# Denominators as jobs on three PSUM banks, register queries staged ahead, bias rows as latent columns, in a two-attention fp32 kernel

## The reference

```
xn = layernorm(h)
# A: latent attention, 8 heads, no mask
c_q, c_kv, k_r = xn@W_DQ + b_DQ, xn@W_DKV + b_DKV, xn@W_KR + b_KR     # 32 columns each
q = [c_q@W_UQ + b_UQ | c_q@W_QR + b_QR];  k = [c_kv@W_UK + b_UK | k_r]
a = softmax(q k^T / sqrt(160));  out_A = (a @ (c_kv@W_UV + b_UV)) @ W_O + b_O
# B: 16 heads of 16, keys masked
q, k, v = xn @ W_qkv
sim = mean over heads of cos(g, q), scaled to 0..1 over all tokens;  pos = sim > 0.9
x_pos, x_neg = attention over the keys with pos / without (the first 5 tokens are keys in both)
rows with pos take x_pos, the others x_neg; the first 5 rows (register) take the mean of both
out = h + out_A + out_B @ W_proj + b_proj
```

## Time and profile before

| | us |
|---|---|
| runs shown (3): lowest, median, highest | 3069.21, 3077.69, 3081.52 |
| profiled execution: its time | 3083.09 |
| its span, first to last instruction | 3081.3 |
| busy: PE, DVE, ACT, POOL | 2900.2, 2256.7, 1676.5, 1428.3 |
| idle of PE ahead of `rs`, until Z was in (8 times) | 14.8 |
| mean granted clock of TensorE (1 is 2.4 GHz) | 0.976 |

### The profile page before, as it was taken

One profiled execution on the slowest core, in us unless ns is written; L12 is line 12 of the kernel. 1 busy time (PEld: TensorE's weight loads), 2 busy tenths in 40 slices (PEclk: granted clock), 3 DMA queues, 4 the chain that ended last, 5 costly groups with the idle time before them and its releaser, 6 DMA issues.

```text
span 3081.3 us, 45461 instructions
## 1 busy us (share of the span) xinstructions
PE 2900.2 (94%) x16898; PEld 1283.4 (42%) x16898; DVE 2256.7 (73%) x4085; ACT 1676.5 (54%) x1947; POOL 1428.3 (46%) x680
## 2 busy tenths in 40 slices
PE   5889999999999999999999999999999999999997
PEld 4634334443344443444334433444434443344433
DVE  5776787767877787767777677777787678776791
ACT  2424565544655566545565456555565456654574
POOL 6649522682227712285225832178122962258301
PEclk9979999998999999999999999999999999999998
DMA  4505234400352024411254003430145112540001
GB/s 148 180 16 98 69 86 99 82 16 30 105 100 62 19 74 97 107 27 34 68 110 89 16 31 92 102 74 20 53 101 114 31 37 63 117 92 16 17 17 36
DMA packets 128485, 211.43 MB, mean 69 GB/s; under 512 B 47560, under 2 KB 76136, under 8 KB 128120
## 3 DMA queue, kind: packets, MB, share of 16 engines
q1 hardware_dynamic: 124160, 201.10, 27.4%
q10 hardware_dynamic: 4104, 7.42, 0.6%
HBM read 136.21 MB, written 71.97 MB: 68 GB/s over the span
## 4 chain that ended last, share of the span: by engine, by line
PE 72%; DVE 13%; DMA 5%; POOL 4%; issue 3%; ACT 1%; SPq 1%; ACTq 0%; POOLq 0%; DVEq 0%
PE O L1207 20%; PE M L1108 12%; PE M L1102 10%; DVE mx L1448 10%; PE S L1192 7%; PE S L1195 6%; PE M L1128 3%; PE M L1172 2%; PE M L1174 2%; PE M L1221 2%; PE M L1140 2%; POOL PTx L734 2%; PE M L1146 1%; DMA recb_d<-RC 1%; DMA RB<-recb_d 1%
## 5 line engine op out<-in xcount | busy, mean ns | idle before, releaser
L1448 DVE TENSOR_REDUCE mx<-M 128x1 f32<-128x512 f32 x3072 | 1972.4, 683 | 567.9 <-PE M L1108 311.2
L956 ACT ACTIVATE PT<-S 128x1024 f32<-128x1024 f32 x1280 | 1241.9, 1022 | 818.5 <-PE S L1195 514.6
L1108 PE MATMUL M<-KB,QB 50*128 50x512 f32 x2048 | 671.3, 480 | 49.2 <-ACT stg L993 14.3
L1108 PEld LDWEIGHTS M<-KB,QB 50*128 50x128 f32 x2048 | 279.9, 185 | 691.6 <-DVE mx L1448 428.4
L1207 PE MATMUL O<-PT,VB 128*32 128x512 f32 x4096 | 554.6, 613 | 0.8 <-ACT PT L956 0.7
L1102 PE MATMUL M<-KA,QA 98*128 98x512 f32 x1024 | 433.0, 469 | 27.1 <-DVE mx L1448 22.0
L1195 PE MATMUL S<-QB,KB 52*128 52x512 f32 x2048 | 380.2, 434 | 6.2 <-DMA QB<-sh_d 2.3
L956 ACT ACTIVATE PTx<-S 128x1024 f32<-128x1024 f32 x256 | 250.2, 1023 | 228.2 <-PE S L1192 218.5
L1102 PEld LDWEIGHTS M<-KA,QA 98*128 98x128 f32 x1024 | 175.6, 191 | 348.8 <-DVE mx L1448 171.4
L1192 PE MATMUL S<-QA,KA 114*128 114x512 f32 x1024 | 316.0, 410 | 0.6 <-DMA QA<-sh_d 0.6
L788 POOL TENSOR_TENSOR PT<-PT,PTx 128x2048 f32<-128x2048 f32 x64 | 292.4, 4568 | 24.0 <-POOL PT L788 13.2
(11 more groups left out here) (153 smaller groups left out, 2120.0 us busy)
## 6 DMA issues: line engine op xcount, KB each, us to landing
qk_d<-stg SPq DMA_DIRECT2D x32, 1024.0 KB
KA<-kt_d SPq DMA_DIRECT2D x48, 512.0 KB, 7.3
QB<-qk_d SPq DMA_DIRECT2D x192, 128.0 KB
KB<-qk_d SPq DMA_DIRECT2D x192, 128.0 KB
kt_d<-stg SPq DMA_DIRECT2D x16, 1024.0 KB
RB<-recb_d SPq DMA_DIRECT2D x64, 256.0 KB
PT<-in_x SPq DMA_DIRECT2D x8, 1024.0 KB, 5.5
RB<-rec_d SPq DMA_DIRECT2D x32, 256.0 KB
```

Of the source, the lines that this page charges most:

```text
L956: nc.scalar.activation(probs(kind, of_a)[:, 2 * pair:2 * pair + 2, :], Sg[pair][:, :].rearrange("p (j s) -> p j s", j=2), ACT.Exp, scale=S ...
L1108: done = mm(m[:, :], QB[rows, 2 * q + a, at:at + P], KB[rows, 2 * q + a, keys], start=True, stop=True)
L1448: v.tensor_reduce(mx[:, g % 2, unit, kh:kh + 1], m[:, :], AX.X, ALU.max).then_inc(free, 1)
```

## The change

- **Denominators.** `denominators` and `take_dens` go. There is a job `dn` for each quad, put first in part 2 of steps 6, 10, ... of A and step 2 of B. It takes the next bank in turn, waits for the sums as before, and VectorE evacuates it: the even quad of a group is copied to DN, the odd one added to it. DN is now in `latT` (SBUF). All stages but the opening and the tail use three banks. `dens` of A waits for the evacuation of the odd quad and reads DN; a copy to DN waits for `den_out` of two groups earlier, and the first `rs` evacuation, whose target `SR` is also in `latT`, for that of A's last group.
- **Z.** Z lies in `stg[:, 1, :]`, 1024 columns wide. For batches 1 to 7 GpSimd clears it at the start of A, after the store of qk3 (`st_out`), and SP loads it in A's group 0, right after `load_b(n, 3)` and ahead of `recs`; for batch 0 both stay in B.
- **Bias rows.** `Wlat` gets 8 more columns, W_lat times `Gb`, made in the opening on the chip (`blat` too). `lat` so gives 104 rows, the last 8 being the bias rows. The jobs, copies and splits of `kb` go; the split `cq` covers 104 rows, its store is two DMAs (cq and kb), and `load_c` also loads kb. `kt0` moves from steps 18, 19 to 20, 21 of B and `kt1` from 28, 29 to 26, 27.

The diff, cut to its core:

```diff
-FILLS = ("cq", "kt0", "kb", "kt1", "qk0", "qk1", "qk2", "qk3")
+FILLS = ("cq", "kt0", "kt1", "qk0", "qk1", "qk2", "qk3")
+LAT = D_LAT + HA
...
-        for at, name in ((18, "kt0"), (24, "kb"), (28, "kt1"), (34, "qk0"), (42, "qk1"), (50, "qk2"), (58, "qk3")):
+        for at, name in ((20, "kt0"), (26, "kt1"), (34, "qk0"), (42, "qk1"), (50, "qk2"), (58, "qk3")):
...
@@ end of jobs_b, then end of jobs_a
+    s[2][2].insert(0, ("dn", QUADS - 1))
...
+    for i in range(QUADS - 1):
+        s[4 * i + 6][2].insert(0, ("dn", i))
...
-        out += [(j, 3 if three is not None and k >= three else 2) for part in step for j in part]
+    return [(j, 3) for step in slots for part in step for j in part]
...
-    DN = M[2]
+    DN = latT[:, :].rearrange("p (i c) -> p i c", i=2)
...
+    with nc.sbuf_tensor("Z", [P, 2 * S], F32R) as z_:
+        Z, Zb = z_[:, S:2 * S], z_[:, S - P:S - P + 2 * QB_ * 144].rearrange("p (i c) -> p i c", c=144)[:, :, P:144]
     stg = sb("stg", [P, 2, S])
...
@@ SP, dens
             if kind == "a":
-                wait_apart(sp, dn_free, n * GA + (g + 1))
-                src = RB[0:P:32, slot, :]
+                spot = dn_spot(n, 2 * g + 1)
+                wait_apart(sp, m_free[spot.bank], spot.upto())
+                src = DN[0:P:32, slot, :]
...
@@ SP, stage A, g == 0
                         load_b(n, 3)
+                        load_z(n)
...
@@ GpSimd
         def clear_z(b):
-            wait_apart(pool, dn_done, b * QUADS + QUADS)
-            nc.gpsimd.memset(Z[:, 0:2 * QB_ * 144].bitcast(F32), 0.0).then_inc(z_clear, 1)
+            wait_apart(pool, st_out, stored(b, NF))
+            nc.gpsimd.memset(Z.bitcast(F32), 0.0).then_inc(z_clear, 1)
...
         def a_steps(n, b, before):
+            if before:
+                clear_z(n)
...
@@ ScalarE
-        def take_dens(n, g):
-            act.wait_ge(dn_done, n * QUADS + 2 * (g + 1))
-            nc.scalar.activation(RB[:, g % 2, :], DN[:, :], ACT.Copy).then_inc(dn_free, 1)
...
@@ TensorE, job
+            elif kind == "dn":
+                pe.wait_ge(summed, n * ADDS + 3 * (j[1] + 1))
+                for jj in range(4):
+                    done = mm(m[32 * jj:32 * jj + 32, :], ones32[:, :], probs("a", 4 * j[1])[:, jj, :],
+                              start=True, stop=True, skip_group_check=True)
...
@@ VectorE, job
+            elif kind == "dn":
+                if odd:
+                    v.tensor_tensor(to, m[:, :], to, ALU.add).then_inc(free, 1)
+                else:
+                    if g >= 2:
+                        dve.wait_ge(den_out, (n * GROUPS + g - 1) * 16)
+                    v.tensor_copy(to, m[:, :]).then_inc(free, 1)
             elif kind == "rs":
...
+                    dve.wait_ge(den_out, (n * GROUPS + GA) * 16)
```

More of the change, by code:

```diff
@@ L68, in prep_jobs @@
     out[9] = [("va", 0)]
-    out[11] = fill_jobs("kb")
-    out[15] = fill_jobs("kt1")
+    out[11] = fill_jobs("kt1")
     for i in range(15):
@@ L140, in jobs_a, with banks @@
             place(s, g * NC, "b", g + 2 - GA)
-    return s
-def banks(slots, three):
-    out = []
-    for k, step in enumerate(slots):
-        out += [(j, 3 if three is not None and k >= three else 2) for part in step for j in part]
-    return out
+    for i in range(QUADS - 1):
+        s[4 * i + 6][2].insert(0, ("dn", i))
+    return s
+def banks(slots):
+    return [(j, 3) for step in slots for part in step for j in part]
 def index(jobs, used=(0, 0, 0)):
@@ L338, in program @@
     NH = B * NC * HB
-    n2, dots, root, newton = [take(NH) for _ in range(4)]
+    n2, dots, root = [take(NH) for _ in range(3)]
+    newton = take(NC * HB)
     xnT2 = take(2 * KD * S).rearrange("p (i k s) -> p i k s", i=2, k=KD)
@@ L457, in fill_rows, with stored @@
     def fill_rows(name):
-        return {"cq": CA, "kb": HA}.get(name, P)
+        return LAT if name == "cq" else P
+    def stored(n, f):
+        return n * ((NF + 1) * 16) + (f + 1 if f else 0) * 16
     block = ctx.enter_context(nc.Block())
@@ L674, in b_steps @@
                 if g == 0:
-                    load_z(b)
+                    if b == 0:
+                        load_z(b)
                     if not last:
@@ L759, in do_split @@
                 if not (b is None and f == 0):
-                    wait_apart(pool, st_out, n * (NF * 16) + f * 16)
+                    wait_apart(pool, st_out, stored(n, f))
             for hf in range(2):
@@ L840, in b_steps @@
             n = b + 1
-            clear_z(b)
+            if b == 0:
+                clear_z(b)
             residual(b, 0)
@@ L943, in exps @@
                 if of_a % 4 == 3:
-                    act.wait_ge(dn_done, n * QUADS + i)
+                    spot = dn_spot(n, i - 1)
+                    act.wait_ge(m_full[spot.bank], spot.upto())
                 else:
@@ L1072, in weights @@
             for h in range(HA):
-                last = mm(M[0][:, 0:D], buvb[:, h, :], Wo[:, h, :], start=(h == 0), stop=(h == HA - 1))
+                mm(M[0][:, 0:D], buvb[:, h, :], Wo[:, h, :], start=(h == 0), stop=(h == HA - 1))
+            for k in range(KD):
+                mm(M[0][:, D + HA * k:D + HA * k + HA], WlatT[0:D_LAT, k * P:(k + 1) * P], Gb[0:D_LAT, :],
+                   start=True, stop=True)
+            last = mm(M[0][D_LAT:LAT, D + HA * KD:D + HA * KD + 1], Gb[:, :], blat_one[:, :], start=True, stop=True)
             last.then_inc(setup_pe, 1)
@@ L1086, in job @@
             kind = j[0]
-            if spot.bank == 2 and spot.fixed in (R0[2], R1[2]):
-                pe.wait_ge(dn_free, b * GA + GA)
-            elif not (spot.b is None and spot.fixed == 0):
+            if not (spot.b is None and spot.fixed == 0):
                 pe.wait_ge(m_free[spot.bank], spot.before())
@@ L1116, in job @@
                 for k in range(KD):
-                    done = mm(m[0:96, :], Wlat[:, k, :], xnT[:, k, j[1] * HALF:(j[1] + 1) * HALF],
+                    done = mm(m[0:LAT, :], Wlat[:, k, :], xnT[:, k, j[1] * HALF:(j[1] + 1) * HALF],
                               start=(k == 0), stop=(k == KD - 1))
-            elif kind in ("kt0", "kt1", "kb"):
+            elif kind in ("kt0", "kt1"):
                 hf = j[1]
@@ L1209, in values @@
             last.then_inc(pv_done, 1)
-        def denominators(n, b, i):
-            g, c = i // 2, i % 2
-            if c == 0:
-                if g == 0 and b is not None:
-                    pe.wait_ge(m_free[2], b * LOOP[2] + U_B[2])
-                elif not (g == 0 and b is None):
-                    pe.wait_ge(dn_free, n * GA + g)
-            pe.wait_ge(summed, n * ADDS + 3 * (i + 1))
-            for jj in range(4):
-                last = mm(DN[32 * jj:32 * jj + 32, :], ones32[:, :], probs("a", 4 * i)[:, jj, :],
-                          start=(c == 0), stop=(c == 1), skip_group_check=True)
-            last.then_inc(dn_done, 1)
         def of_batch(j, n, b):
-            own = j[0] in ("mb", "rs", "rt", "rv", "po") or (j[0] == "fa" and j[1] == "b")
+            own = j[0] in ("mb", "dn", "rs", "rt", "rv", "po") or (j[0] == "fa" and j[1] == "b")
             return b if own else n
@@ L1272, in a_steps @@
                     values(b, STEPS_B - 1, "b")
-                if k >= 6 and k % 4 == 2:
-                    denominators(n, b, (k - 6) // 4)
                 some(k, 2)
@@ L1386, in weights @@
             own.settle()
-            v.tensor_tensor(cst[:, :], M[0][:, 0:D], bo, ALU.add).then_inc(setup_dve, 1)
+            own.link(v.tensor_copy(Wlat[:, :, D_LAT:LAT], M[0][:, D:D + HA * KD].rearrange("p (k h) -> p k h", k=KD)))
+            own.link(v.tensor_copy(blat[D_LAT:LAT, :], M[0][D_LAT:LAT, D + HA * KD:D + HA * KD + 1]))
+            own.link(v.tensor_tensor(cst[:, :], M[0][:, 0:D], bo, ALU.add))
+            own.settle()
+            dve.sem_inc(setup_dve, 1)
         def cosines(b):
@@ L1461, in job @@
                 if b is not None and j[1] == 0:
-                    own.link(v.memset(latT[96:97, :], 1.0))
+                    own.link(v.memset(latT[D_LAT:P, :], 1.0))
                     own.settle()
-                v.tensor_scalar(latT[0:96, cols], m[0:96, :], blat[:, 0:1], None, ALU.add).then_inc(free, 1)
+                v.tensor_scalar(latT[0:LAT, cols], m[0:LAT, :], blat[:, 0:1], None, ALU.add).then_inc(free, 1)
             elif kind == "va":
```

108 lines of the change are left out of this document (53 added, 55 removed).

## The result

| | before | after |
|---|---|---|
| median of 4 runs | 3079.61 us (3069.21 to 3083.36) | 2947.57 us (2945.65 to 2948.73) |
| span of the profiled execution | 3081.3 us | 2946.9 us |

The ratio is 0.9576, with a 95% interval of 0.9551 to 0.9600: the changed kernel is 4.2% faster. The forecast was 3.5%.

The account below looks back on a forecast made before the run. PE was taken as the bound, losing 0.45 us per plain step of A to two banks, GpSimd next. Terms of -107.5 us took 3083.1 to 2975.6; the median, 5.4 lower, gave 2970 us, 8-in-10 range 2940 to 3025.

Parts of the forecast that it names:

- GpSimd is what A will wait for, 123.8 us of sums: Stage A: GpSimd's sums set its length, 130.5 us to the last denominators in place of 139.8, gain 9.3 a batch.
- 2.5 us a batch for the clock behind PE's wait: End of A: PE's wait for GpSimd lowers its granted clock, costing 2.5 us a batch, bounds 0 to 5.
- PE's floor, 32 steps x 0.45 us less: Stage A: the third bank saves PE 14.4 us over 32 steps, giving PE a floor of 124.2 us.
- Batch 0, 3 us: Stage A of batch 0: only slack between GpSimd's last sum and the denominators gained, 3 us, bounds 0 to 5.
- VectorE's evacuations +2.4, B's step 3 -4.8: The last set's evacuation in B costs 2.4 us; B's step 3 goes from 3.30 to 2.70, -4.8 over 8 batches.
- Z, -21.7; kb's jobs and the stall, -32.4: Stage B: waits for Z and slow `rs` bursts go, -21.7 us; kb's jobs -11.4; the staging copies' stall -21.
- The opening, -1: Opening: one GpSimd split fewer, three small matmul groups more, -3 to +2 us, taken as -1.
- 1: Stage A: PE's waits spoil its clock and A keeps its length, 3020 us; chance 0.15.
- 2: Stage B: the staging chain's stall moves to qk0, 2991 us; chance 0.10.
- 3: Stage A: Z's loads ahead of `recs` on SP land RB late and GpSimd pays, 2998 us; chance 0.08.
- 4: Stage A: VectorE's in-order queue keeps PE where it is despite the third bank, no gain, 3020 us; chance 0.05.
- 5: Stage A: PE alternates waiting for GpSimd and running at 1.2 GHz, slower than before, 3136 us; chance 0.04.

Follow-up runs that it names:

- lump: Changed kernel plus 12 clearings of an unused tile on GpSimd ahead of the sums of A's last quad, every batch: 2981.66 us.
- spread kernel: Changed kernel plus 2 clearings of an unused tile on GpSimd ahead of every quad of A: 2999.39 us.
- two_banks: Changed kernel with stage A's jobs, denominators included, on two banks in turn in place of three: 3048.03 us.
- denominators alone: Kernel before with only A's denominators as jobs on three banks in turn, taken out by VectorE: 2990.53 us, ratio 0.9699.
- bias rows alone: Kernel before with only the bias rows as 8 more latent columns, no kb job, kt1 following kt0: 3042.01 us, ratio 0.9867.
- kt1's old slot: Changed kernel with kt1's jobs of the preparation back in slot 15 in place of 11: 2942.72 us.

## Why the prediction was right, and where its sum was off

The working went by 3083.1 us to 2975.6; the profiled execution of the changed kernel, 1.8 us around its span of 2946.9 included, took 2948.7, 27 us less. By its steps:

- **GpSimd is what A will wait for, 123.8 us of sums: right.** They take 122.9 to 123.3 us in batches 1 to 7, start 6.3 us after the first scores (5.8 forecast), and the end is 129.3 to 129.7 us (130.5 forecast). Timeline of GpSimd in the same batch, the first sum and the last:

```profile
1251.89 4.60 POOL L802 TENSOR_TENSOR PT<-PT 128x2048 f32<-128x2048 f32 x1 [6.82 <-ACT PT L973]
...
1370.27 4.54 POOL L802 TENSOR_TENSOR PTx<-PTx 128x2048 f32<-128x2048 f32 x1 [0.27 <-POOL PTx L802]
```

  The lump and the spread kernel show the bound at its slope of 1, two_banks that the third bank is what moves PE out of the way.
- **2.5 us a batch for the clock behind PE's wait: the step that failed.** The prediction took PE's slack of 6.3 us as a wait "most of it in front of the last denominators". PE had 1.3 to 2.0 us of slack, not 6.3, so no wait at this place was longer than 1.16 us, and in six of the batches 1 to 7 the clock did not fall there. The first window covers A in one of the six, then come three at its end, and last one of batch 6, whose last denominators start at 2400.37:

```profile
1245.60:1375.60 130.00, 126.78 (x692) 61.48 (x690) 102.37 (x179) 70.57 (x75) 118.10 (x30) 1.00 0.16 37
1364.40:1369.40 5.00, 4.03 (x28) 1.54 (x28) 4.51 (x10) 2.54 (x3) 4.73 (x2) 1.00 0.04 3
1369.40:1374.40 5.00, 3.62 (x25) 0.92 (x17) 4.05 (x8) 3.77 (x4) 4.73 (x2) 1.00 0.13 51
1374.40:1379.40 5.00, 4.35 (x28) 1.69 (x30) 3.10 (x6) 1.94 (x2) 0.41 (x1) 1.00 0.02 5
...
2399.00:2412.00 13.00, 12.25 (x50) 4.67 (x47) 6.98 (x11) 4.25 (x6) 1.23 (x1) 0.50 0.22 70
```

  What follows the last denominators takes 214.6 us in batch 6 and 210.3 in the batches without a slow stretch, so this one fall cost 4.3 us, 0.6 a batch over the seven. The term is 17.5 of the 27 us; the prediction had kept 0 as its lower bound, and in six batches 0 it was. By the lump it would have been next to 0 even with a wait of 3 us and a fall to 0.50, as long as the slow stretch is over by about the end of GpSimd's last sum.
- **PE's floor, 32 steps x 0.45 us less: wrong, without effect on A's length.** A plain step went from 3.42 to 2.98 us, forecast 2.97. But A's first scores to B's fell by 11.0 us, 0.34 a step: the 0.45 of a plain step was multiplied by all 32, and steps that carry other jobs gained less (a step of 3.41 us stayed at 3.41, one of 5.32 became 4.80). It had no effect on A's length because GpSimd was later anyway, by much less than believed; its one effect was the clock term above.
- **Batch 0, 3 us: measured 7.3.** The bounds were 0 to 5, from the slack behind the last sum alone. That slack gave 1.1 us; the first sum starts 2.4 us sooner, and the sums take 131.4 us in place of 135.3, since an idle time of GpSimd of 3.8 us among them is gone, where the prediction had it hardly idle.
- **VectorE's evacuations +2.4, B's step 3 -4.8.** The step went from 3.30 to 2.89 in its median, so -3.3 for the two of them, forecast -2.4. What was costed at nothing, den_d's store going earlier, had a user after all: Z's transfers stand behind it on SP, and with the denominators alone most of PE's wait for Z was gone.
- **Z, -21.7; kb's jobs and the stall, -32.4; together -56.5 with the terms above: measured -57.1.** Every `rs` burst is now undisturbed (the chain, to be laid beside the earlier trace rows):

```profile
358.28 3.87 PE M L1161 x16
...
2416.85 3.88 PE M L1161 x16
```

  That the total is so close is in part luck. Step 6 gave 23.4 us, close to Z's term, though the denominators would have given nearly as much without Z. Steps 18 to 29, which hold kb's jobs and the stall, gave 25.4 us where 32.4 were put down; the other 8.3 us are spread over the other steps, step 3 among them. With the bias rows alone these steps gave 30.1. The split between jobs and stall was off as well: steps 24 to 26 went from 10.4 to 9.9 us, not to 8.75, since kt1's jobs now stand there; steps 28 and 29 together went from 8.2 to 11.7 us before to 4.9 after.
- **The opening, -1: measured +4.2**, of which some 3 are given back by kt1's old slot; two openings that differ by no edit lay nearly as far apart (193.4 and 196.6).
- **The rivals.** 1: in A of batches 1 to 7 the clock stayed at 1.00 but for the last 1.7 us of batch 6, and A became shorter by its 10 us. The Trainium skill, "TensorE: Matmul & The Clock Gate", section "A second HAM failure mode: psum-queue depth-cycling", tells of a kernel in which a PE that cycles through PSUM banks idles briefly often enough to swing between its two clocks. For stage A of the changed kernel the trace doesn't agree, three banks in turn at 1.00; at its end one batch in seven shows a fall to 0.50 with no wait longer than 0.90 us ahead of it, and in the spread kernel five of seven do, behind waits of up to 1.51 us. 2: in B no staging copy waits for a store any more. 3: GpSimd goes from sum to sum with gaps of 0.27 us and at most 0.56, no RB comes late inside A. 4: refuted by two_banks, which is how such a kernel looks. 5: needed a slow clock through A.

Of the 27 us, 17.5 are the clock, 9 what A ended sooner than 130.5 us (130.5 to 129.5, 7 times, would be 7; some of it is the 139.8 that stood for batches of up to 141.0), 4 batch 0 and 1 the rest of B (with batch 6's 4.3 us of clock in it), less 5 for the opening.

## What to carry to other kernels

When a bank or buffer is freed, ask which engine is next, and compute its floor from its own instructions and their gaps: that number was right within 1 us, while the floor of the engine that is given the resource was 3 to 4 us too low, because a plain step stood for all. A lower clock costs only where the slow stretch outlasts the event that the engine would wait for anyway; put a price on it only after asking what comes last. And an edit that moves a store earlier on an in-order DMA queue moves everything queued behind it: look there before it is costed at nothing.

## What the runs showed of the hardware that was not expected

- At the end of A the granted clock stayed at 1.00 through waits of 0.90, 0.36 to 0.42, 0.41 and 1.15 us in six batches of the changed kernel, and fell to 0.50 in the seventh behind waits of 0.90, 0.65 and 0.41 us. Waits of 0.90, 0.41 and 1.51 us (spread) were followed by 0.50 in five batches and by 1.00 in one; waits of 0.90 and 3.02 to 3.33 us (lump) came with 0.50 in all seven, from within the longer wait on in six of them and from 0.2 us behind it in one.
- GpSimd's sum of 128x2048 takes 4.50 to 4.61 us in every kernel, though VectorE's busy time in A rose from 92.5 to 102.4 of 130 us: the two did not slow each other in a measurable way.
- Two profiled executions whose openings differ by no edit differ by 3 us at A's first scores (193.4 and 196.6); the difference arises where the granted clock is 0.50 for 10 us in one of them and 1.00 in the other.
